# TensorE's order in a step of a two-layer graph network: half message sums between and behind the next pair's two groups of products

## The chip, the cores and the metric

The kernel runs on one core of a Trainium2 chip. The metric is the device time of one execution in microseconds; before the change it is 1939.5 us, the median of three runs (1931.52 to 1940.32). Engines are called PE (TensorE), ACT (ScalarE), DVE (VectorE), POOL (GpSimd) and SP (SyncE, which issues DMAs).

## The reference

There are 6250 nodes with 128 features and 100000 edges, sorted by target, with 16 features each. Two layers follow each other. Cut to what matters:

```
# layer one, over edges e = (src, dst)
m    = silu(concat(h[src], h[dst], edge_feat) @ W1 + b1) @ W2 + b2
agg  = segment_sum(m, dst)                       # per target node
hnew = silu(concat(h, agg) @ W3 + b3) @ W4 + b4
x1   = layernorm(x + (hnew + h))
# layer two
z    = (1 + eps) * x1 + segment_sum(x1[src], dst)
z    = relu(z @ V1 + c1) @ V2 + c2
y    = relu(layernorm(z + x1) * gamma + beta)
out  = layernorm(x1 + y)
```

## The kernel before

**Tiling.** Edges are cut into 196 groups of 512 (`GE`, four chunks `CH` of 128), and two groups make a pair: 98 pairs. A pair's targets lie within a window of 128 nodes (`PW`), because edges are sorted by target. A unit is 128 nodes; there are 48 units, the last one with two tiles. Layer one first computes the source term `x @ W1[:128] + b1` of all nodes and keeps it in HBM (`A_d`, "src_term"), so that an edge only has to fetch a row.

**A pair in layer one.** POOL gathers the source rows, one indirect DMA (`gather_rows`, L873) for each chunk: four for a group, eight for a pair. They go to a ring of eight group slots, `gath`; a slot is free when PE has read the group that was in it (`pool.wait_ge(pre_ps, done(g - RING))`, L888). The first four groups are gathered from `x` instead. DVE makes two one-hots: `terms_l` for target and edge features (`windows`, L1914, one instruction for each group, counted by `ohT_made`), and `oh` for the sums (`one_hots`, L1644). ACT fills the other halves of the operands (`edge_features`, L1006). PE adds up a group's inputs in a bank (`pre_sums`, L1224: four products L1233, then the gathered rows through a product with the identity, L1240), which it counts in `pre_ps`; ACT takes the SiLU of it (`messages`, L1017, counted by `msg_made`); PE sums the messages by target (`message_sums`, L1242: eight products L1250 into bank 2 or 3, then the degrees, L1252, counted by `sums_ps`); DVE adds the window into `S` (`add_sums`, L1927, instruction L1934).

[...]

**Steps.** Every engine runs the same staggered steps (`steps`, L477): in step s an engine does each of its stages for pair s minus the stage's lag, in the order in which the stages are listed. Four steps form a loop body; steps at the ends, and those that do something special, are written out. PE's list stands at L1514 to L1520: in step s it does `turn_ef` of pair s-1, `pre_sums` of pair s-2, then the early work, then `message_sums` of pair s-3, then the units' matmuls (`ordered_turn_x1`, `ordered_out0`, `ordered_hidden0`) for units whose targets are complete.

**Beside layer one.** Over steps 1 to 43 DVE also sorts the edges of the first 112 groups by source, with short transposes by PE (`turn_keys`). From step 45 on the early work begins: a part of layer two is done for tiles that are finished. PE has `early_sums` (L1396, target sums) and `early_rows` (L1383, choosing rows out of loaded windows), DVE `early_hots` (L1987 and L1993), SP the window loads.

**Units.** The unit's hidden layer, output, mean and variance (`rows0`, L2046: L2052, L2056, `stats`), inverse root and normalisation (L2036) follow 7 to 11 steps behind. ACT computes the root for all units but the last one, for which POOL computes it (`rsqrt0`, L913), queued behind all gathers. The rows go to HBM (`layer1_input`).

**The passage to layer two.** POOL gathers two more pairs' worth of rows ("bridge", 16 indirect DMAs) for finished tiles, then the last unit's root, and then waits until all of x1 is stored: `pool.wait_ge(x1_out, landed(NT - 1))` (L933). In layer two POOL gathers 42 pairs (336 indirect DMAs), PE chooses and sums rows (L1410, L1434, L1362) and does the node matmuls (L1441, L1456), and DVE builds one-hots, adds, and normalises.

**What PE waits for in the two stages at issue.** `pre_sums` waits for `efT_made` of the pair, for both windows of the pair (`ohT_made, done(2 * k + 1)`), for the SiLU that frees the bank (`msg_made, done(g - 2)`) and for the gathered rows. `message_sums` waits for the one-hots `oh_made`, for the addition two pairs before (`sums_added`), and for the messages of each half.

Of the kernel before, what the change touches and what calls it, by code (L numbers as in the profile page):

```python
# [14 lines left out]
D = 128  # L15
FE = 16
CH = 4
GE = CH * P
W = 64
PW = 2 * W  # L20
# [23 lines left out]
def done(n):  # L44

    return n + 1 + START
# [11 lines left out]
def build(nc, x, src, dst, ef, W1, b1, W2, b2, W3, b3, W4, b4, eps, V1, c1, V2, c2, gamma, beta, out):  # L58
# [36 lines left out]
    with ExitStack() as ctx:  # L95
        def sb(name, shape, dt=F32):
            return ctx.enter_context(nc.sbuf_tensor(name, shape, dt))
# [6 lines left out]
        def counter(name, engine):  # L104

            counters.setdefault(engine, []).append(sem(name))
            return counters[engine][-1]


        ident = sb("ident", [P, P])  # L110
# [83 lines left out]
        deg_col = sb("deg_col", [P, DEEP])  # L194
        ef_s = sb("ef_s", [P, 2, 2 * CH * FE])
        oh = sb("oh", [P, 2, 2 * CH, PW])
        pre = sb("pre", [P, CH * D])
        msg = sb("msg", [P, 4, CH * D])
# [14 lines left out]
        bank = [ctx.enter_context(nc.psum_tensor(f"bank{i}", [P, 512], F32)) for i in range(8)]  # L213
# [112 lines left out]
        ohT_made = counter("ohT_made", "dve")  # L326
        oh_made = counter("oh_made", "dve")
        xw_made = counter("xw_made", "act")
        ef_turned = counter("ef_turned", "pe")
        efT_made = counter("efT_made", "act")  # L330
        pre_ps = counter("pre_ps", "pe")
        msg_made = counter("msg_made", "act")
        sums_ps = counter("sums_ps", "pe")
        deg_added = counter("deg_added", "dve")
        sums_added = counter("sums_added", "dve")
# [78 lines left out]
        def of_pair(lag, body):  # L414

            return lag, NPAIR, body

        def of_unit(lag, body):

            def at_even(i, m, q):  # L420
                if m % 2 == 0:
                    body(i // 2 if isinstance(i, int) else q * 2 + m // 2)
            return lag, 2 * UNITS, at_even

        def of_early(lag, body):

            return lag + FIRST_EARLY, EARLY, body
# [94 lines left out]
        def at_steps(parts):  # L522

            return 0, NPAIR, only_at(parts)
# [99 lines left out]
        def of_unit_in(first, last, lag, body):  # L624

            count, _, part = last - first, None, of_unit(0, lambda j: body(first + j))[2]
            return lag + 2 * first, 2 * count, part
# [11 lines left out]
        UNITS = NT - 1  # L639
# [3 lines left out]
        FIRST_BEFORE = (FIRST_EARLY + 3 - 8) // 2  # L643
# [486 lines left out]
        def _(pe):  # L1130
            start_counters(pe, "pe")
            mm = nc.tensor.matmul
# [82 lines left out]
            def add_from_x(g, ps):  # L1215

                pe.wait_ge(from_x_kept, g + 1)
                for j in range(CH):
                    mm(ps[:, j * D:(j + 1) * D], gath[:, g, j * P:(j + 1) * P], wab[:, 0:D], start=False, stop=False)
                for j in range(CH):  # L1220
                    last = mm(ps[:, j * D:(j + 1) * D], ident[:, :], b1_bc[:, :], start=False, stop=j == CH - 1)
                last.then_inc(pre_ps, 1)

            def pre_sums(k, m, q):  # L1224

                u = m % 2
                pe.wait_ge(efT_made, done(k))
                pe.wait_ge(ohT_made, done(2 * k + 1))
                for h in range(2):
                    g = 2 * k + h  # L1230
                    pe.wait_ge(msg_made, done(g - 2))
                    for j in range(CH):
                        mm(bank[h][:, j * D:(j + 1) * D], terms_l[:, u, h, j, :], terms_r[:, u, h, j, :],  # L1233
                           start=j == 0, stop=False)
                    if isinstance(k, int) and k < FROM_X:
                        add_from_x(g, bank[h])
                        continue
                    slot = 2 * m + h
                    pe.wait_ge(gathered[slot], 16 * CH * (q + 1))
                    mm(bank[h][:, :], ident[:, :], gath[:, slot, :], start=False, stop=True).then_inc(pre_ps, 1)  # L1240

            def message_sums(k, m, q):  # L1242
                u = m % 2

                pe.wait_ge(oh_made, done(k))
                pe.wait_ge(sums_added, done(k - 2))
                for c in range(2 * CH):
                    if c % CH == 0:
                        pe.wait_ge(msg_made, done(2 * k + c // CH))
                    mm(bank[2 + u][:, 0:PW], msg[:, 2 * u + c // CH, c % CH * D:(c % CH + 1) * D], oh[:, u, c, :],  # L1250
                       start=c == 0, stop=c == 2 * CH - 1)
                mm(bank[2 + u][0:1, PW:2 * PW], deg_col[:, m:m + 1], ident[:, :],  # L1252
                   start=True, stop=True).then_inc(sums_ps, 1)

            def hidden0(j, turned, run=0):

# [243 lines left out]
            def any_order():  # L1500
                for x in range(BRIDGED):
# [10 lines left out]
                all_units1(pe, hidden1, out1)  # L1512

            steps(pe, NPAIR - 2, (4,) + TURNS + tuple(s + 1 for s in TURNS) + (SORTED, SORTED + 1),  # L1514
                  of_early(3, early_kept), of_pair(1, turn_ef), of_pair(2, pre_sums), of_early(3, early_sums),
                  of_early(2, early_rows), (0, NPAIR, keys_taken),
                  of_unit_in(FIRST_BEFORE, UNITS - 1, 9, hnew_read), of_pair(3, message_sums),
                  at_steps({4: weight_products, **{k + 1: lambda k=k: turn_from_x(k) for k in range(FROM_X)}}),
                  of_unit(10, ordered_turn_x1), *in_banks(8, ordered_out0), of_unit(7, ordered_hidden0),
                  (0, NPAIR, turn_keys))  # L1520
# [677 lines left out]
```

## Time and profile before

| what | value |
|---|---|
| median of three runs | 1939.5 us (1931.52, 1939.5, 1940.32) |
| span of the profiled execution | 1500.6 us |
| own time of the profiled execution | not given; the runs lie 430.9 to 439.7 us above the span |
| PE busy | 1285.9 us, 86% |
| POOL busy | 1107.0 us, 74% |
| DVE busy | 1014.5 us, 68% |
| ACT busy | 642.1 us, 43% |
| mean granted clock of PE | 0.945 of full speed |

The span runs from the first to the last instruction of the profiled execution; what lies around it in a timed run is start and end of the program. Layer one's loop takes up the span to about 1035 us, layer two the rest. A busy share counts an engine's instructions alone; matmuls are pipelined and their ends modelled, so that starts are firmer than ends. POOL's own rows are the indirect DMAs' issue: the gathered bytes land later. "issue" is idle time in which an engine waited for nothing that the profile shows.

### The profile page before, as it was taken

How to read it: one execution, taken by the hardware profiler on the slowest of the kernel's cores; microseconds unless marked ns; L12 is line 12 of the kernel's file. 1: busy time of each engine (PE TensorE's matmuls, PEld its weight loads, DVE VectorE, ACT ScalarE, POOL GpSimd, SP SyncE). 2: the span in 40 equal slices, each digit the busy share in tenths (PEclk: the TensorE clock that was granted, in tenths of full speed). 3: DMA queues.
4: the chain of work that ended last, by engine and by line, in shares of the span. 5: the costliest groups of instructions: out<-in, count | busy, mean ns of one | idle time of the engine just before them, and what ended most of it. 6: DMA issues, size and time to landing. Idle time of an engine off the chain costs nothing.

```text
span 1500.6 us, 31339 instructions
## 1 busy us (share of the span) xinstructions
PE 1285.9 (86%) x8165; PEld 1063.6 (71%) x8165; DVE 1014.5 (68%) x2310; ACT 642.1 (43%) x1257; POOL 1107.0 (74%) x1164
## 2 busy tenths in 40 slices
PE   6788789778777889888888888885999999999992
PEld 6666667556556667767767776764899999998982
DVE  4678888677665565665566656643666888878866
ACT  2744556555555555555556555551111111111111
POOL 5777777777777777777777777777777777777771
PEclk9898889999998999999999999997999999999996
DMA  6533333333336454454455445433887778778731
GB/s 206 135 85 92 93 95 94 95 96 91 95 90 119 118 138 125 126 136 131 125 131 133 125 128 135 113 80 105 258 261 230 208 230 241 222 230 241 213 92 47
DMA packets 189124, 214.15 MB, mean 143 GB/s; under 512 B 60426, under 2 KB 149517, under 8 KB 189011
## 3 DMA queue, kind: packets, MB, share of 16 engines
q1 hardware_dynamic: 138399, 131.62, 28.9%
q0 software_dynamic: 36352, 74.52, 21.3%
q10 hardware_dynamic: 14260, 6.68, 1.6%
q8 instruction: 49, 0.80, 0.2%
q14 instruction: 64, 0.52, 0.1%
HBM read 202.74 MB, written 9.85 MB: 142 GB/s over the span
## 4 chain that ended last, share of the span: by engine, by line
POOL 42%; PE 32%; issue 15%; DVE 4%; DMA 4%; SPq 1%; ACT 1%; DVEq 0%; ACTq 0%; POOLq 0%
POOL gath L873 42%; PE bank L1434 9%; PE bank L1410 8%; PE bank L1362 4%; DMA gath<-src_term,src_col 2%; PE bank L1240 2%; PE bank L1250 2%; PE bank L1233 2%; PE bank L1421 1%; DMA T<-in_x 1%; DMA gath<-layer_input,src_col 1%; PE bank L1396 1%; PE bank L1383 1%; PE bank L1441 0%; PE bank L1456 0%
## 5 line engine op out<-in xcount | busy, mean ns | idle before, releaser
L873 POOL DMA_INDIRECT gath<-src_term,src_col x768 | 737.2, 960 | 234.2 <-issue 230.2
L873 POOL DMA_INDIRECT gath<-layer_input,src_col x336 | 329.6, 981 | 105.6 <-issue 100.6
L1240 PE MATMUL bank<-gath,ident 128*128 128x512 f32 x384 | 218.3, 652 | 114.5 <-DMA gath<-src_term,src_col 113.8
L1233 PEld LDWEIGHTS bank<-terms_r,terms_l 128*128 128x128 f32 x1568 | 209.4, 201 | 83.1 <-issue 69.2
L1233 PE MATMUL bank<-terms_r,terms_l 128*128 128x128 f32 x1568 | 219.6, 286 | 30.4 <-ACT msg L1022 22.0
L1923 DVE TENSOR_SCALAR_CACHE_REDUCE terms_l<-dst_bc,node_col 64x512 f32<-64x512 int32 x196 | 221.0, 1128 | 13.1 <-issue 7.2
L1250 PEld LDWEIGHTS bank<-oh,msg 128*128 128x128 f32 x1568 | 198.7, 202 | 26.9 <-issue 26.1
L1934 DVE TENSOR_TENSOR S<-S,bank 128x128 f32 x98 | 28.1, 286 | 270.2 <-PE bank L1252 178.2
L1250 PE MATMUL bank<-oh,msg 128*128 128x128 f32 x1568 | 202.3, 285 | 0.0
L1434 PE MATMUL bank<-S 128*128 128x288 f32 x672 | 170.0, 406 | 0.1
L1649 DVE TENSOR_TENSOR oh<-bank,dst_rel 128x1024 f32<-128x1024 f32 x140 | 169.8, 1213 | 0.0
L1240 PEld LDWEIGHTS bank<-gath,ident 128*128 128x128 f32 x384 | 61.2, 201 | 129.7 <-DMA gath<-src_term,src_col 129.4
L1434 PEld LDWEIGHTS bank<-S 128*128 128x128 f32 x672 | 124.5, 190 | 31.1 <-issue 0.2
L1022 ACT ACTIVATE msg<-bank 128x512 f32<-128x512 f32 x196 | 115.8, 599 | 59.8 <-PE bank L1240 57.4
L1013 ACT COPY terms_l<-bank 64x512 f32<-64x512 f32 x196 | 113.7, 580 | 40.0 <-PE bank L1203 28.6
L1076 ACT COPY S<-bank 128x512 f32<-128x512 f32 x84 | 49.2, 586 | 185.8 <-PE bank L1410 181.8
L1993 DVE TENSOR_TENSOR S<-bank,dst_of 128x2304 f32<-128x2304 f32 x44 | 112.0, 2548 | 10.1 <-PE bank L1434 3.8
L1014 ACT COPY terms_r<-bank 64x512 f32<-64x512 f32 x196 | 113.4, 578 | 0.0
L1035 ACT ACT_TABLE_LOAD x48 | 61.6, 1283 | 66.9 <-DVE mv L2025 66.4
L1362 PE MATMUL bank<-oh,gath 128*128 128x128 f32 x672 | 84.4, 279 | 5.1 <-DMA gath<-layer_input,src_col 5.1
L1362 PEld LDWEIGHTS bank<-oh,gath 128*128 128x128 f32 x672 | 80.4, 195 | 5.7 <-DMA gath<-layer_input,src_col 5.7
L1987 DVE TENSOR_SCALAR xT<-xT,even_odd 128x1024 f32<-128x1024 f32 x84 | 60.5, 762 | 5.4 <-DMA xT<-sorted_src 5.4
(219 smaller groups left out, 1754.7 us busy)
## 6 DMA issues: line engine op xcount, KB each, us to landing
dst_bc<-in_dst SPq DMA_DIRECT2D x195, 128.0 KB
xT<-sorted_src SPq DMA_DIRECT2D x42, 512.0 KB
xs<-layer_input SPq DMA_DIRECT2D x136, 128.0 KB
gath<-src_term,src_col POOLq DMA_INDIRECT x768
terms_l<-layer_input SPq DMA_DIRECT2D x88, 128.0 KB
terms_r<-layer_input SPq DMA_DIRECT2D x88, 128.0 KB
msg<-layer_input SPq DMA_DIRECT2D x80, 128.0 KB
ef_s<-in_edge_attr SPq DMA_DIRECT2D x97, 64.0 KB
```

The costliest lines, as they stand in the source:

```text
L873: g.indirect_dma_start(out=to[:, j * D:(j + 1) * D], out_offset=None, in_=table[0:rows, :], in_offset=bass.IndirectOffsetOnAxis(ap=indices ...
L1013: a.copy(terms_l[r, u, h, :, :], bank[4][r, 0:P].unsqueeze(1).to_broadcast([W, CH, P]))
L1014: last = a.copy(terms_r[r, u, 1 - h, :, :], bank[4][r, P:2 * P].unsqueeze(1).to_broadcast([W, CH, P]))
L1022: a.activation(msg[:, 2 * (m % 2) + h, :], bank[h][:, :], ACT.Silu).then_inc(msg_made, 1)
L1233: mm(bank[h][:, j * D:(j + 1) * D], terms_l[:, u, h, j, :], terms_r[:, u, h, j, :], start=j == 0, stop=False)
L1240: mm(bank[h][:, :], ident[:, :], gath[:, slot, :], start=False, stop=True).then_inc(pre_ps, 1)
L1250: mm(bank[2 + u][:, 0:PW], msg[:, 2 * u + c // CH, c % CH * D:(c % CH + 1) * D], oh[:, u, c, :], start=c == 0, stop=c == 2 * CH - 1)
L1362: last = mm(bank[2 + u][:, 0:PW], gath[:, s, c % CH * D:(c % CH + 1) * D], oh[:, u, c, :], start=c == 0, stop=c == 2 * CH - 1)
L1410: last = mm(bank[h][:, c * D:(c + 1) * D], src_hot[:, u, w, e], x_near[m][h * CH + c][:, w, :], start=w == 0, stop=w == 1)
L1434: last = mm(bank[4][:, 0:DW], rows_kept[:, c // CH, c % CH * D:(c % CH + 1) * D], dst_hot[:, u, c, :], start=o % LATE == 0 and c == 0, sto ...
L1649: ve_.tensor_tensor(oh[:, u, :, :], iota_ps.unsqueeze(1).to_broadcast(shape), dst_rel[:, ds((k + first) * (2 * CH), 2 * CH)].unsqueeze(2). ...
L1923: ve_.tensor_scalar(terms_l[r, u, h, :, :], dst_bc[r, u, :].rearrange("n (p j) -> n j p", j=CH), node_col[r, ds(k, 1)], None, ALU.is_equal ...
```

## The change

In `message_sums` the eight products of a pair are split into two bodies, one for each half (group) of the pair, and so is `pre_sums`, one for each group. The order in a step becomes: `pre_sums` of group 0, the early work, half 0 of the sums of the pair before, `pre_sums` of group 1, half 1 of these sums with the degrees. The waits go along: `efT_made` is now waited for by each of the two groups; a group waits for its own window only (`ohT_made, done(g)`); `oh_made` and `sums_added` stand before half 0. The matmuls and their operands are the same.

```diff
-            def pre_sums(k, m, q):
-                u = m % 2
-                pe.wait_ge(efT_made, done(k))
-                pe.wait_ge(ohT_made, done(2 * k + 1))
-                for h in range(2):
+            def pre_sums(h):
+                def body(k, m, q):
+                    u = m % 2
                     g = 2 * k + h
+                    pe.wait_ge(efT_made, done(k))
+                    pe.wait_ge(ohT_made, done(g))
                     pe.wait_ge(msg_made, done(g - 2))
...
-            def message_sums(k, m, q):
-                u = m % 2
-                pe.wait_ge(oh_made, done(k))
-                pe.wait_ge(sums_added, done(k - 2))
-                for c in range(2 * CH):
-                    if c % CH == 0:
-                        pe.wait_ge(msg_made, done(2 * k + c // CH))
-                    mm(bank[2 + u][:, 0:PW], msg[:, 2 * u + c // CH, c % CH * D:(c % CH + 1) * D], oh[:, u, c, :],
-                       start=c == 0, stop=c == 2 * CH - 1)
-                mm(bank[2 + u][0:1, PW:2 * PW], deg_col[:, m:m + 1], ident[:, :],
-                   start=True, stop=True).then_inc(sums_ps, 1)
+            def message_sums(h):
+                def body(k, m, q):
+                    u = m % 2
+                    if h == 0:
+                        pe.wait_ge(oh_made, done(k))
+                        pe.wait_ge(sums_added, done(k - 2))
+                    pe.wait_ge(msg_made, done(2 * k + h))
+                    for j in range(CH):
+                        mm(bank[2 + u][:, 0:PW], msg[:, 2 * u + h, j * D:(j + 1) * D], oh[:, u, h * CH + j, :],
+                           start=h == 0 and j == 0, stop=h == 1 and j == CH - 1)
+                    if h == 1:
+                        mm(bank[2 + u][0:1, PW:2 * PW], deg_col[:, m:m + 1], ident[:, :],
+                           start=True, stop=True).then_inc(sums_ps, 1)
+                return body
...
-                  of_early(3, early_kept), of_pair(1, turn_ef), of_pair(2, pre_sums), of_early(3, early_sums),
+                  of_early(3, early_kept), of_pair(1, turn_ef), of_pair(2, pre_sums(0)), of_early(3, early_sums),
                   of_early(2, early_rows), (0, NPAIR, keys_taken),
-                  of_unit_in(FIRST_BEFORE, UNITS - 1, 9, hnew_read), of_pair(3, message_sums),
+                  of_unit_in(FIRST_BEFORE, UNITS - 1, 9, hnew_read), of_pair(3, message_sums(0)),
+                  of_pair(2, pre_sums(1)), of_pair(3, message_sums(1)),
```

## Rows read from the trace of the kernel before

**Rows 1.** The page: busy time of the engines, and the chain that ended last

```profile
PE 1285.9 (86%) x8165; PEld 1063.6 (71%) x8165; DVE 1014.5 (68%) x2310; ACT 642.1 (43%) x1257; POOL 1107.0 (74%) x1164
...
POOL 42%; PE 32%; issue 15%; DVE 4%; DMA 4%; SPq 1%; ACT 1%; DVEq 0%; ACTq 0%; POOLq 0%
```

**Rows 2.** Waits of POOL, whole span: total us, times, longest

```profile
POOL gath L873 <- issue: 335.4, 1100, 0.3
...
POOL gath L873 <- PE bank L1240: 4.0, 13, 0.3
POOL gath L873 <- DMA layer_input<-ot: 3.5, 1, 3.5
```

**Rows 3.** Stretches, gathers alone: length, POOL busy (count), granted clock, DMA share, GB/s

```profile
900.00:1000.00 100.00, 75.91 (x80) 0.98 0.44 115
...
1100.00:1200.00 100.00, 76.18 (x78) 1.00 0.78 232
```

**Rows 4.** Timeline of POOL, layer one's ends: start, duration [idle before <-releaser]

```profile
22.49 1.15 POOL L873 DMA_INDIRECT xs<-in_x,src_col  x1 [5.89 <-DVE src_col L1536]
...
1013.41 1.01 POOL L873 DMA_INDIRECT gath<-src_term,src_col  x1 [0.30 <-issue]
...
1033.73 0.96 POOL L873 DMA_INDIRECT gath<-layer_input,bridge_rows  x1 [0.30 <-issue]
1034.72 0.25 POOL L918 TENSOR_SCALAR var_eps<-mv 128x2 f32<-128x2 f32 x1
...
1039.28 1.08 POOL L873 DMA_INDIRECT gath<-layer_input,src_col  x1 [3.49 <-DMA layer_input<-ot]
```

**Rows 5.** Timeline of PE, one step of layer one

```profile
802.66 1.05 PE L1233 MATMUL bank<-terms_r,terms_l 128*128 128x128 f32 x8
804.97 1.13 PE L1240 MATMUL bank<-gath,ident 128*128 128x512 f32 x2 [1.25 <-DMA gath<-src_term,src_col]
805.93 1.13 PE L1396 MATMUL bank<-src_rows_f,As 128*128 128x288 f32 x4
806.90 1.05 PE L1383 MATMUL bank<-xs,xTs 128*128 128x128 f32 x8
807.79 1.95 PE L1250 MATMUL bank<-oh,msg 128*128 128x128 f32 x16
809.67 0.38 PE L1252 MATMUL bank<-ident,deg_col 128*1 128x128 f32 x2
```

**Rows 6.** Timelines of PE and POOL, where the ring of gather slots is tightest

```profile
80.17 1.78 PE L1240 MATMUL bank<-gath,ident 128*128 128x512 f32 x2
...
93.78 0.96 POOL L873 DMA_INDIRECT gath<-src_term,src_col  x1 [0.30 <-issue]
```

**Rows 7.** Waits of PE, whole span

```profile
PE bank L1240 <- DMA gath<-src_term,src_col: 113.8, 71, 10.6
```

**Rows 8.** Timeline of all engines, end of layer one

```profile
1016.11 1.29 PE L1240 MATMUL bank<-gath,ident 128*128 128x512 f32 x2 [3.17 <-DMA gath<-src_term,src_col]
1017.19 3.46 PE L1250 MATMUL bank<-oh,msg 128*128 128x128 f32 x16
...
1031.98 0.25 DVE L2025 BATCH_NORM_AGGREGATE mv<-st 128x2 f32<-128x6 f32 x2
```

**Rows 9.** Timelines of POOL and DVE, two gathers longer than most

```profile
177.31 1.26 POOL L873 DMA_INDIRECT gath<-src_term,src_col  x1 [0.30 <-issue]
...
177.45 0.28 DVE L2052 SCALAR_TENSOR_TENSOR v<-xt,b_bc 128x128 f32<-128x128 f32 x1
...
810.98 0.61 DVE L1987 TENSOR_SCALAR xTs<-As,even_odd 128x256 f32<-128x256 f32 x2
...
811.12 1.05 POOL L873 DMA_INDIRECT gath<-src_term,src_col  x1 [0.30 <-issue]
```

**Rows 10.** Timelines of PE and POOL, first neighbour sums of layer two

```profile
1071.36 1.95 PE L1362 MATMUL bank<-oh,gath 128*128 128x128 f32 x16
...
1080.70 0.95 POOL L873 DMA_INDIRECT gath<-layer_input,src_col  x1 [0.30 <-issue]
```

More of the change, by code:

```diff
@@ L1236, in pre_sums @@
                         add_from_x(g, bank[h])
-                        continue
+                        return
                     slot = 2 * m + h
@@ L1240, in pre_sums @@
                     mm(bank[h][:, :], ident[:, :], gath[:, slot, :], start=False, stop=True).then_inc(pre_ps, 1)
-            def message_sums(k, m, q):
-                u = m % 2
-                pe.wait_ge(oh_made, done(k))
-                pe.wait_ge(sums_added, done(k - 2))
-                for c in range(2 * CH):
-                    if c % CH == 0:
-                        pe.wait_ge(msg_made, done(2 * k + c // CH))
-                    mm(bank[2 + u][:, 0:PW], msg[:, 2 * u + c // CH, c % CH * D:(c % CH + 1) * D], oh[:, u, c, :],
-                       start=c == 0, stop=c == 2 * CH - 1)
-                mm(bank[2 + u][0:1, PW:2 * PW], deg_col[:, m:m + 1], ident[:, :],
-                   start=True, stop=True).then_inc(sums_ps, 1)
+                return body
[12 more added lines that the diff above has]
+                           start=True, stop=True).then_inc(sums_ps, 1)
+                return body
             def hidden0(j, turned, run=0):
```

## The prediction

> **What bounds the kernel now.** I read the page first. Its busy shares point at TensorE: PE is busy 86% of the span, POOL 74%. The chain that ended last says otherwise: POOL holds 42% of it, PE 32% [rows 1], and "issue" 15%. So the question is which of the two would let the other go faster, and that is asked stage by stage.
>
> POOL's waits come second. Of its idle time, 335.4 us in 1100 pieces is "issue", the fixed 0.3 us between two gathers; only 4.0 us in 13 pieces is put down to PE, and none of those is over 0.3 us, the fixed gap again [rows 2]. The reader is to see that POOL never stands still for PE in layer one.
>
> The stretches confirm it: 80 gathers in 100 us of layer one [rows 3]. POOL's timeline gives the whole stage: the first gather starts at 22.49 and the last of the bridge ends at 1033.73 + 0.96 = 1034.69, after 800 gathers (16 from x, 768 of the source term, 16 of the bridge) [rows 4]. That is 1012.2 us / 800 = 1.265 us each, against 0.96 + 0.30 = 1.26 for one undisturbed gather. POOL is a conveyor that runs without a stop from before layer one's loop until layer two opens. A pair is 8 gathers, 10.1 us.
>
> PE's own waits are the mirror image: 113.8 us in 71 pieces before L1240, for gathered rows [rows 7]. PE is ahead of its supply and waits for the conveyor.
>
> Then layer two. After the last bridge gather POOL makes the last unit's inverse root (L918 at 1034.72), VectorE normalises, the rows are stored, and the next gather starts at 1039.28, released by that store [rows 4]. Nothing before that moment but POOL's queue sets it: the variance that POOL needs was ready at 1031.98 + 0.25 = 1032.23 [rows 8], 2.46 us before POOL came free.
>
> **The change, part by part.** In a step TensorE now does: products and gathered rows of group 0 of pair k; the early work; sums of half 0 of pair k-1; products and rows of group 1 of pair k; sums of half 1 of pair k-1 and the degree row.
>
> *Matmuls.* None is added or removed. Per pair there remain 16 products, 4 rows instructions, 16 sum instructions and 2 for the degree; half a message sum is 1.95 / 2 = 0.98 us [rows 5].
>
> *Waits.* Today a pair's products and sums issue 6 + 4 = 10 waits, then 8 + 4 = 12. Two more per step are not shown anywhere as work. The lower bound is 0. The upper bound is, by the nearest row, POOL's pause of 0.30 at each gather [rows 4]: 0.6 us a step. I take 0, because PE stands 1.25 us in that step before the gathered rows of group 1 [rows 5], and 0.6 fits in it. Without that cover it would be at most 98 x 0.6 = 59 us; PE's total wait of 113.8 [rows 7] is larger.
>
> *Order in a steady step* [rows 5]. Now PE finishes group 1's products by 803.7, waits until the rows land at 804.97, and only then does rows (0.96 start to start), early sums and early rows (0.97 + 0.89), message sums (1.88) and degree (0.38): 5.08 us behind the landing, at 810.05. Then the early work and 0.98 of sums stand ahead of the wait, and behind the landing come only 0.96 + 0.98 + 0.38 = 2.3 us. VectorE's addition of the sums is released some 2.8 us sooner. PE's work per 10.1 us stays the same, so the same 1.25 us is left over and still ends with a landing. The step's period is the conveyor's. Worth at the end of the span: 0.
>
> *Group 1 of a pair is read later when PE is not waiting for rows.* Its slot and its bank come free behind early work and half a sum: 0.97 + 0.89 + 0.98 = 2.8 us later in the step. Queued behind: POOL's gather eight groups later, ScalarE's SiLU of that group, and VectorE's windows. The ring has eight groups, and the tightest place I found is at group 14: its gather starts at 93.78, the read that freed its slot (group 6's) ended at 80.17 + 1.78 = 81.95 [rows 6], 11.83 us earlier. 2.8 us uses a quarter of that, so POOL does not notice: 0. Lower bound 0 as well, for POOL has nothing to gain from a slot freed sooner.
>
> *Narrower waits.* Group 0's products now need only the first window one-hot of the pair, not both, but half 0 of the sums, and with it group 1, needs pair k-1's one-hots, which stand behind both windows in VectorE's queue. The one gives PE about a window, the other takes about that back. All of it lies under the ring's 11.83 us. 0.
>
> *The tail.* The last layer-one rows land at 1016.11; behind them stand L1240 (1.29) and the sums of pair 96 (3.46, against 1.95 in the steady step) [rows 8, 5]. Half of the latter moves ahead into the 3.17 us that PE waited: 0.98 to 1.73 us sooner for the variance that POOL takes. It is already 2.46 us early, so the gain is 0, and the margin becomes about 4 us. If instead all of the tail's matmuls ran as slowly as these sums, the variance could come late, and what exceeds 2.46 us would count; I allow 0 to 2 us.
>
> *Layer two.* Its code is the same. POOL's first slot wait there has 1080.70 - (1071.36 + 1.95) = 7.39 us to spare [rows 10], and POOL again issues 78 gathers in 100 us [rows 3]. Nothing to gain or lose but the start.
>
> **A rule that speaks against the change.** POOL's time per gather isn't quite constant. The gather at 177.31 took 1.26 us with L2052, a VectorE instruction on two SBUF inputs, beginning inside it; the one at 811.12 took 1.05 with L1987 beginning 0.14 before it [rows 9]; the usual is 0.96. The whole excess in layer one is small: 1034.69 - 22.49 - 800 x 1.26 = 4.2 us. The change moves VectorE's instructions against the gathers. [...] Bounds from rows: all excess gone, -4.2 us; every one of the 49 units' L2052 costing 1.26 - 0.96 = 0.30 and every one of the 48 early steps' L1987 costing 0.09, 14.7 + 4.3 = +19 us. I take 0, since the phase is as arbitrary after as before.
>
> **Sum.** 0 (matmuls) + 0 (waits) + 0 (order) + 0 (ring) + 0 (tail) + 0 (layer two) on a span of 1500.6 us. No time of its own is given with the profiled execution; the three timed runs lie 1931.5 - 1500.6 = 430.9 to 439.7 us above its span. So a span of 1500.6, and 1939.5 us against the median.
>
> **Rivals.**
> *PE is the bound* (faster). For it: 86% busy, and the 71 waits before L1240. If each of these hid a half sum of 0.98 us that is serial today, 71 x 0.98 = 69.6 us, 1870 us. Against it: POOL's gaps never exceed 0.3 us, so no gather could start earlier.
> *Gathers stretched by VectorE* (slower). The mechanism above; its addition follows the landing at a new phase, which repeats every pair, so a bad phase would repeat too. Full price +19 us, 1958.5; from half of that on (9.7 us) it decides. Against: 800 gathers show 4.2 us in all.
> *The ring runs dry* (slower). In the steps with the sort, VectorE and PE are late by themselves, and if the new order lengthened a step by 0.5 us over the 40 steps up to about 460 us, 20 us of lag less 11.83 of slack would be 8 us on POOL, 1947.7; over 0.54 us a step it passes 9.7. Against: PE's total is unchanged and its results for VectorE come sooner.
> That the change doesn't do what it says is excluded: the two halves stand in TensorE's program order.
>
> **Numbers.** About 0.5%, 9.7 us, is what a measurement can tell from no change; the three runs alone spread 8.8 us. Forecast 0.88. PE-bound 0.03. Stretched gathers 0.04. Ring 0.02. A shift that no row explains 0.03, of which faster 0.02. Stretching and ring are slower by over 0.5% in most of their cases; together with the unexplained: faster 0.05, same 0.88, slower 0.07. Range: from the lowest run less 1.5, 1930, up to 1946, which is the highest run plus some 6 us of stretching.
>
> **What would show it.** Right: 80 gathers per 100 us from 100 to 1000 us, no POOL gap over 0.31 before the store of layer one's last rows, the last bridge gather ending near 1034.7, layer two's first gather near 1039.3; L1250 in two blocks of 8 per step; the addition L1934 some 2 to 3 us nearer the landing; PE's wait before L1240 similar in sum. Wrong: POOL waiting on PE for over 0.3 us at a time, many gathers over 1.0 us, or L918 starting later than POOL came free.

## The result, and the profile after

The changed kernel takes 1878.4 us (median of 4 runs, 1873.41 to 1883.44) beside 1937.2 us (median of 4, 1931.52 to 1940.32) of the kernel before: a ratio of 0.972, with a 95% interval from 0.969 to 0.975. The forecast was 1939.5 us and no change.

The first thing to see lies outside the rows. The profiled execution of the changed kernel took 1873.41 us by its own time and has a span of 1871.5 us: they differ by 1.9 us. The trace of before has a span of 1500.6 us, while its timed runs take 1931.5 to 1940.3. If the same 1.9 us hold for the kernel before, the missing 431 to 440 us never lay around the span, and that trace is of another kind of execution of the same program. The next section shows that this is so: a long execution of the kernel before has a span of 1942.8 us in a time of 1944.7. I call the two kinds *short* (about 1500 us) and *long* (about 1900 us).

The page of the changed kernel, a long execution (busy us and share, then the chain that ended last), answers to [rows 1]:

```profile
PE 1446.5 (77%) x8165; PEld 1158.7 (62%) x8165; DVE 1016.3 (54%) x2310; ACT 630.6 (34%) x1257; POOL 1103.6 (59%) x1164
...
another core or an unknown queue 27%; issue 21%; PE 20%; DVE 20%; DVEq 7%; ACT 3%; SPq 1%; ACTq 1%; DMA 1%; POOLq 0%; POOL 0%
```

Its waits of POOL over the span (us in total, times, longest) answer to [rows 2]:

```profile
POOL gath L873 <- issue: 287.5, 938, 0.9
POOL gath L873 <- remote: 203.3, 119, 3.4
POOL gath L873 <- PE bank L1366: 122.2, 37, 24.6
POOL gath L873 <- PE bank L1240: 50.2, 24, 4.5
```

Its gathers alone by stretch (length, POOL busy and count, granted clock, DMA share, GB/s) answer to [rows 3]:

```profile
200.00:300.00 100.00, 62.94 (x67) 0.73 0.27 75
900.00:1000.00 100.00, 60.45 (x64) 0.92 0.37 103
1500.00:1600.00 100.00, 63.45 (x65) 0.96 0.61 182
```

And POOL's timeline where layer two opens answers to [rows 4]:

```profile
1267.14 0.23 POOL L918 TENSOR_SCALAR var_eps<-mv 128x2 f32<-128x2 f32 x1 [18.75 <-DVE mv L2030]
...
1271.68 1.08 POOL L873 DMA_INDIRECT gath<-layer_input,src_col  x1 [3.49 <-DMA layer_input<-ot]
```

From 900 to 1000 us a gather still takes 60.45 / 64 = 0.94 us, but there are 64 in 100 us and not 80. POOL is no longer a conveyor: 50.2 us of waiting for L1240 in 24 pieces of up to 4.5 us, where [rows 2] has 4.0 us in 13 pieces of 0.3, and 203.3 us in 119 pieces for "remote", a releaser that the trace doesn't name. Layer two's first gather starts at 1271.68, against 1039.28 in [rows 4]. PE's busy sum has grown from 1285.9 to 1446.5 us with the same 8165 instructions. Nothing of this can be put down to the change, because the two traces are of different kinds. For that a long trace of the kernel before was needed.

### The profile page after: what moved, and what is told of

The parts are those of the page before. It is cut to its first block, busy times and chain, and to the rows that moved or that the text cites. A ratio compares the mean times of both kernels' runs of the same rounds, so it can differ in the third digit from the quotient of the medians.

```text
span 1871.5 us, 31423 instructions
## 1 busy us (share of the span) xinstructions
PE 1446.5 (77%) x8165; PEld 1158.7 (62%) x8165; DVE 1016.3 (54%) x2310; ACT 630.6 (34%) x1257; POOL 1103.6 (59%) x1164
## 4 chain that ended last, share of the span: by engine, by line
another core or an unknown queue 27%; issue 21%; PE 20%; DVE 20%; DVEq 7%; ACT 3%; SPq 1%; ACTq 1%; DMA 1%; POOLq 0%; POOL 0%
DVEq L1934 5%; DVE terms_l L1928 4%; PE bank L1438 4%; DVE oh L1654 4%; PE bank L1252 3%; PE bank L1414 2%; PE bank L1233 2%; PE bank L1240 2%; DVE bank L1741 2%; DVE src_rows_f L1745 1%; PE bank L1366 1%; DVE src_rows_f L1749 1%; ACT S L1076 1%; DVE st L2025 1%
## 5 line engine op out<-in xcount | busy, mean ns | idle before, releaser
L1252 PEld LDWEIGHTS bank<-oh,msg 128*128 128x128 f32 x1568 | 234.9, 219 | 152.4 <-issue 120.1
L1233 PE MATMUL bank<-terms_r,terms_l 128*128 128x128 f32 x1568 | 256.2, 307 | 63.9 <-issue 48.3
L1252 PE MATMUL bank<-oh,msg 128*128 128x128 f32 x1568 | 242.4, 303 | 61.9 <-issue 35.7
L1233 PEld LDWEIGHTS bank<-terms_r,terms_l 128*128 128x128 f32 x1568 | 228.2, 219 | 71.4 <-issue 69.7
L1240 PE MATMUL bank<-gath,ident 128*128 128x512 f32 x384 | 229.1, 678 | 14.2 <-issue 13.9
L1022 ACT ACTIVATE msg<-bank 128x512 f32<-128x512 f32 x196 | 113.5, 596 | 324.3 <-remote 229.2
L1438 PE MATMUL bank<-S 128*128 128x288 f32 x672 | 194.7, 448 | 25.1 <-ACT S L1076 22.0
L1438 PEld LDWEIGHTS bank<-S 128*128 128x128 f32 x672 | 138.6, 212 | 72.2 <-issue 32.6
L1366 PE MATMUL bank<-oh,gath 128*128 128x128 f32 x672 | 104.3, 290 | 57.0 <-issue 55.3
L1387 PE MATMUL bank<-xs,xTs 128*128 128x128 f32 x384 | 66.6, 328 | 80.9 <-issue 55.2
L1387 PEld LDWEIGHTS bank<-xs,xTs 128*128 128x128 f32 x384 | 59.8, 234 | 100.5 <-issue 98.5
L1240 PEld LDWEIGHTS bank<-gath,ident 128*128 128x128 f32 x384 | 68.4, 219 | 26.2 <-issue 26.1
```

The costliest lines, as they stand in the source:

```text
L1022: a.activation(msg[:, 2 * (m % 2) + h, :], bank[h][:, :], ACT.Silu).then_inc(msg_made, 1)
L1252: mm(bank[2 + u][:, 0:PW], msg[:, 2 * u + h, j * D:(j + 1) * D], oh[:, u, h * CH + j, :], start=h == 0 and j == 0, stop=h == 1 and j == CH ...
L1366: last = mm(bank[2 + u][:, 0:PW], gath[:, s, c % CH * D:(c % CH + 1) * D], oh[:, u, c, :], start=c == 0, stop=c == 2 * CH - 1)
L1387: last = mm(rows_early_ps[:, c * D:(c + 1) * D], hot_early[:, u, w, c * P:(c + 1) * P], near_early[:, u, c, w, :], start=w == 0, stop=w == 1)
L1438: last = mm(bank[4][:, 0:DW], rows_kept[:, c // CH, c % CH * D:(c % CH + 1) * D], dst_hot[:, u, c, :], start=o % LATE == 0 and c == 0, sto ...
```

## The comparison in long executions: where the 59 us lie

Both kernels ran again, unchanged. The first time they met only short executions (`b_again` and `a_again`, below). The second time, on another chip, both were long.

> The kernel before, unchanged, on another chip. If the long executions (1937 us) belong to a chip or to a stretch of time, this run can meet them: then its time is near 1937, its span lies within 3 us of its time, and its trace shows how its TensorE stalls, late releases and gathers stand against those of the changed kernel's long execution. Otherwise it comes out at 1499 to 1503 us as the runs so far, and the cause of the 0.972 stays open.

> The changed kernel, unchanged, beside b_third. Where before takes 1937, both theories of a gain that belongs to the long executions expect 1870 to 1885 (ratio 0.97). Where before takes 1500, all theories expect 1499 to 1503 (ratio 0.999 to 1.001).

Measured: before 1944.7 us in this run, with a span of 1942.8, and 1941.79 in the median of the 7 runs beside it (1938.53 to 1950.03). The changed kernel takes 1886.22 (median of 4, 1881.4 to 1891.17), a ratio of 0.9717 [0.9675, 0.9759]. The gain repeats, and it belongs to long executions.

The page of the kernel before in its long execution (as above):

```profile
PE 1466.9 (76%) x8165; PEld 1174.0 (60%) x8165; DVE 1019.0 (52%) x2310; ACT 631.4 (32%) x1257; POOL 1100.5 (57%) x1164
...
another core or an unknown queue 28%; PE 25%; issue 20%; DVE 12%; ACT 6%; DVEq 3%; SPq 2%; ACTq 2%; DMA 1%; POOLq 0%; POOL 0%
```

Its gathers by stretch:

```profile
200.00:300.00 100.00, 64.42 (x67) 0.83 0.28 76
900.00:1000.00 100.00, 55.50 (x58) 0.91 0.35 96
1500.00:1600.00 100.00, 60.27 (x63) 0.95 0.59 175
```

Those of the changed kernel, beside it on the same chip:

```profile
200.00:300.00 100.00, 64.66 (x67) 0.86 0.28 76
900.00:1000.00 100.00, 62.27 (x66) 0.94 0.40 108
1500.00:1600.00 100.00, 59.65 (x62) 0.95 0.59 174
```

Read the three lines as three stages. From 200 to 300 us, before there is any early work, both issue 67 gathers. In layer two both are alike, 63 and 62. From 900 to 1000 the kernel before issues 58 and the changed one 66. Counted by the degree rows, one burst for each pair: pairs 3 to 42 take 12.08 us each before and 12.10 after; pairs 48 to 92 take 13.83 before and 12.29 after, 44 x 1.54 = 68 us. Pair 48 comes at 670 before and at 676 after, the last pair at 1322 and 1264; from there to the end both need 621 and 617 us. So the gain is made in the steps that have early work (64 us from pair 48 to the last one), and outside them little changes: 6 us are lost ahead of pair 48 and 4 gained behind the last pair.

What TensorE waits for in that stretch (engine, instruction, releaser: us in total, times, longest), first of the kernel before, 700 to 1300 us:

```profile
PE bank L1201 <- issue: 45.5, 18, 5.1
PE bank L1233 <- issue: 39.9, 49, 1.9
PE bank L1201 <- ACT As L1068: 34.2, 7, 6.3
```

Then of the changed kernel, 700 to 1250 us:

```profile
PE bank L1387 <- issue: 40.2, 25, 2.8
PE bank L1233 <- issue: 27.9, 48, 1.2
...
PE bank L1387 <- ACT terms_r L1014: 9.6, 6, 6.1
...
PE bank L1201 <- issue: 0.5, 2, 0.3
```

L1201 is the first matmul of a step. Ahead of it TensorE's program has `early_kept`, a wait for ScalarE's copy (L1068) of the early rows that TensorE itself made in the step before: the copy must be done before their bank is written again. Before, 34.2 + 45.5 = 79.7 us pass there (I count "issue" in, as a releaser of which the trace has no record, for long executions have few records of signals, see the end; for a single wait that is not shown). After, 0.5 us. One such step of the kernel before, in TensorE's timeline (start, duration, instruction [idle before <-releaser]; each product of these lines is two rows in the trace, so x16 is eight products):

```profile
887.63 0.27 PE L1233 MATMUL bank<-terms_r,terms_l 128*128 128x128 f32 x1 [0.45 <-issue]
...
891.18 1.13 PE L1383 MATMUL bank<-xs,xTs 128*128 128x128 f32 x8
892.15 1.95 PE L1250 MATMUL bank<-oh,msg 128*128 128x128 f32 x16
...
894.98 0.48 PE L1262 MATMUL bank<-T,cdeg 1*128 x2
901.40 0.47 PE L1201 MATMUL bank<-ident,ef_s 128*128 128x128 f32 x1 [5.94 <-ACT As L1068]
```

and ScalarE's copy between them:

```profile
900.78 0.37 ACT L1068 COPY As<-bank 128x256 f32<-128x256 f32 x1 [5.36 <-remote]
```

The early rows (L1383) end at 891.18 + 1.13 = 892.31. ScalarE then has other work until 895.42, stands idle for 5.36 us and starts the copy only at 900.78, 8.47 us after the rows. The trace also records when a semaphore was counted, and it has the count of these rows at 900.75: what came late is the signal. Behind the rows TensorE has the message sums, the degree row and a unit's matmuls, which last until 894.98 + 0.48 = 895.46. Then it stands 5.94 us. In the changed kernel the same part of a step reads:

```profile
889.73 1.13 PE L1387 MATMUL bank<-xs,xTs 128*128 128x128 f32 x8 [0.79 <-issue]
...
892.48 1.02 PE L1240 MATMUL bank<-gath,ident 128*128 128x512 f32 x2
...
895.28 0.48 PE L1266 MATMUL bank<-T,cdeg 1*128 x2
895.98 0.30 PE L1201 MATMUL bank<-ident,ef_s 128*128 128x128 f32 x1 [0.22 <-issue]
```

```profile
894.70 0.37 ACT L1068 COPY As<-bank 128x256 f32<-128x256 f32 x1
```

The early rows (L1387) end at 889.73 + 1.13 = 890.86 and are copied at 894.70, 3.84 us later; their count stands at 893.72, 2.86 us behind them, and ScalarE had a SiLU to finish first. Group 1's products and rows (the second line is its L1240) and the halves of the sums now lie behind them, so that TensorE is busy until 895.28 + 0.48 = 895.76 and waits 0.22 us. The cover behind the early rows was 895.46 - 892.31 = 3.15 us and is 895.76 - 890.86 = 4.90, which is 1.75 us more: one group's products and rows, 891.59 to 893.35.

Theory K, formed from this: in long executions a signal of TensorE reaches its reader late (from the end of the early rows to the copy: median 3.0 and up to 8.5 us before, 1.9 and up to 5.3 after, over 48 steps each, against a median of 0.04 in the short execution of before). The early rows' way to ScalarE and back is then longer than what TensorE has to do meanwhile, and the loop of the two sets the step. The new order would help because it moves the early rows ahead by a group.

Theory K is not the whole of it, and two readings of the same traces show that. The first is ScalarE's waits (us in total, times, longest). The kernel before, 700 to 1300 us:

```profile
ACT As L1068 <- remote: 122.7, 22, 9.7
ACT msg L1022 <- remote: 2.7, 1, 2.7
```

The changed kernel, 700 to 1250 us:

```profile
ACT msg L1022 <- remote: 200.7, 54, 7.8
ACT As L1068 <- remote: 5.6, 1, 5.6
```

ScalarE waited for the early rows before and waits for a group's gathered rows (the SiLU, L1022) after. The recorded counts say the same: from pair 48 to 94, the count of group 0's rows (L1240) stands a median of 0.01 us behind their end before, and 4.85 us after. So the new order does not only put more work behind a late signal; other signals are late in it. Why, no run shows.

The second reading is where TensorE stands idle for over 0.3 us, from the degree row of pair 48 to that of the last pair, by the idle times that the profile gives. These pauses sum up to 155 us before and 109 after, while the stretch is 652 us long before and 588 after. At the head of the step (L1201) 89.0 us became 0.3. But before the early rows (L1383, now L1387) 3.8 became 51.5, and before the early sums (L1396, now L1400) 18.1 came up from nothing: of the 89 us some 66 came back there. At the products and gathered rows (L1233 and L1240) 55.9 became 30.2, most of it inside bursts in which nothing is waited for. The other 18 us of the 64 are no pauses: TensorE's instructions themselves take up 19 us less (494 and 475). So the head of the step, less what came back, is 23 us of 64, about a third.

## The experiments

Theory L, the first, said that a shorter loop of TensorE is what pays when TensorE is the bound. Theory S said that late signals of TensorE in general favour the new order. Their rival was that nothing but noise or the condition differs.

**Both kernels unchanged, first time.** No edit.

> The kernel before, unchanged, for a second profile. Theory of the prediction (the profiled execution shown is what is timed, and 439 us lie outside its span): span near 1500 us, POOL without a gap over 0.31 us in layer one, and a time near 1937 us. Theory B (the timed executions run otherwise than the one whose trace was read; the changed kernel's span lies only 1.9 us under its time): span near 1935 us, about 12.9 us per pair in layer one against 10.1, POOL standing still at the first gather of each group for a freed slot, additions of the sums (L1934) starting 3 to 5 us behind the degree row (L1252) where the first trace has 0.14.

> The changed kernel, unchanged, beside the others on one chip. Both theories: 1873 to 1884 us, span 2 us less, 12.3 us per pair in steady steps of layer one, ratio 0.972.

Measured: `b_again` 1499.06 us with a span of 1497.2, and before 1500.64 (25 runs, 1498.4 to 1503.59); `a_again` 1500.55 (10 runs), a ratio of 1.0004 [0.9994, 1.0013]. No theory had expected these times. In short executions the change is worth nothing. POOL's waits in `a_again`:

```profile
POOL gath L873 <- issue: 338.5, 1111, 0.3
...
POOL gath L873 <- PE bank L1366: 1.2, 4, 0.3
```

1111 pauses of the fixed 0.3 us, and not one for L1240: the conveyor of the forecast, unchanged by the new order.

**Parts of the change.** `c_waits` has the split bodies and waits in the old order; `c_whole` puts group 1 behind both halves.

```diff
 c_waits: pre_sums(0), pre_sums(1), early_sums, early_rows, ..., message_sums(0), message_sums(1)
 c_whole: pre_sums(0), early_sums, early_rows, ..., message_sums(0), message_sums(1), pre_sums(1)
```

> Split bodies with the waits of the change, but in the order of before: group 0, group 1, early work, half 0, half 1. If the narrower waits (a group's own window) make the gain: 1878 us, ratio 0.97. If the order makes it: 1937 us, ratio 1.00 within 0.003.

> Group 1 behind both halves of the message sums, which stay together: group 0, early work, half 0, half 1 with degrees, group 1. If the gain comes from the two groups being apart (ScalarE, POOL and VectorE get one result each half step): about the changed kernel's 1878 us or better, ratio 0.97 or less. If it comes from sums standing on both sides of group 1: at most half of it, 1905 us or more. If my conveyor were the bound: 1937.

Measured: 1501.17 (ratio 1.0002 [0.9993, 1.0012]) and 1500.45 (1.0004 [0.9995, 1.0014]). Both were short executions, in which none of these orders matters. They say nothing of the long ones.

**POOL's bound taken away.** Two of the four chunks of a group are gathered, and the other two are left out, so that half of the gathered rows are stale.

```diff
-                for j in range(CH):
+                for j in range(chunks):
...
-                    gather_rows(A_d, N, g % RING, src_col[:, g * CH:(g + 1) * CH], gathered[g % RING])
+                    gather_rows(A_d, N, g % RING, src_col[:, g * CH:(g + 1) * CH], gathered[g % RING], chunks=2)
```

> The kernel before, but in layer one POOL gathers only two of a group's four chunks, so that half of the gathered rows are stale: it leaves out half of the gathers, which makes the conveyor 5.05 us per pair. PE's own work, about 8.8 us a pair, and the loops between the engines are then the bound. Both theories: layer one some 100 to 130 us shorter, 1370 to 1410 us where the kernel before takes 1500.

> The changed kernel with the same half of the gathers left out. Theory L (the new order shortens the loop between PE and the engines that wait for it, and this is hidden only where POOL is the bound): 0.6 us a pair less than the other, which is what 1937 against 1878 us makes, so about 50 to 60 us below it. Theory P (the order is worth nothing to PE's throughput; its gain needs signals of PE that arrive late): within 8 us of it.

Measured: 1368.16 us in the old order (ratio 0.9119 [0.9103, 0.9134]), 1391.43 in the new one (0.9267 [0.925, 0.9285]). The old order comes out just under the expected 1370 to 1410. With TensorE's side as the bound the new order is 23 us *slower*, which neither theory expected. A pair takes 8.63 against 8.99 us (pairs 48 to 92, from the degree rows). TensorE's waits in the new order, 500 to 850 us, hold one that the old order doesn't have:

```profile
PE bank L1400 <- DVE T L1962: 11.9, 9, 1.4
```

The early sums (L1400) wait for VectorE (L1962), now that they come one group's work sooner. That is the price side of the same move, and from pair 48 to 92 most of it: TensorE stands idle 0.29 us a pair there in the new order and never in the old one. Theory L falls.

**TensorE lengthened.** Every L1233 and L1250 product is made twice.

```diff
-                    for j in range(CH):
-                        mm(bank[h][:, j * D:(j + 1) * D], terms_l[:, u, h, j, :], terms_r[:, u, h, j, :],
+                    for again_ in range(2):
+                        for j in range(CH):
+                            mm(bank[h][:, j * D:(j + 1) * D], terms_l[:, u, h, j, :], terms_r[:, u, h, j, :],
```

> The kernel before with each product of L1233 and L1250 made twice, which doubles these terms: 32 more rows of 0.11 us a pair, 3.5 us, so that PE needs 12.3 us a pair against POOL's 10.1. Both theories: 1700 to 1740 us, with POOL standing still for freed slots in layer one.

> The changed kernel with the same products made twice. Theory L: 40 to 60 us below the other one. Theory P: within 8 us, for PE is then busy without a pause in either order.

Measured: 1640.13 (1.093 [1.091, 1.095]) and 1641.61 (1.0944 [1.0925, 1.0963]), both below the 1700 to 1740 that were expected: a pair takes the expected 12.2 us from pair 48 to 92, but only 10.4 from pair 3 to 42, where there is no early work yet. TensorE is the bound where there is, and POOL waits for it in 78 places of `p_old`:

```profile
POOL gath L873 <- PE bank L1241: 136.4, 78, 2.8
```

Yet the order is worth nothing. From pair 48 to 92 TensorE has no idle gap in either order, and a pair takes 12.19 us in both, as theory P said; theory L falls again.

**Three signals late.** The counts `ef_turned`, `pre_ps` and `sums_ps` go by SyncE, which reads TensorE's own count, moves 64 bytes, waits for them and only then counts (`ef_turned` without the 64 bytes).

```diff
+            def relay(raw, out, per_pair, h, turn):
+                def body(k, m, q):
+                    sp.wait_ge(raw, done(per_pair * k + h))
+                    if turn is not None:
+                        sp.dma_start(relayed[:, :], x[0:1, 0:16]).then_inc(relay_in, 16)
+                        sp.wait_ge(relay_in, relay_count(k, turn))
+                    sp.sem_inc(out, 1)
+                return body
```

> The kernel before, with TensorE's signals in layer one made late: the counts of L1203, L1240 and the degree row go to SyncE, which passes them on; ahead of passing on a group's rows or a pair's sums it makes a 64 byte DMA and waits for it, some 2 us. Matmuls, gathers and order are the kernel's own. Theory S (what the recorded times of 1937 and 1878 us have in common is late signals of TensorE, and the old order suffers more from them): a pair takes over 10.1 us, POOL stands still for freed slots, 1550 to 1950 us. Theory N (late signals are hidden by the ring of eight groups): 1500 to 1520.

> The changed kernel with the same late signals. Theory S: 0.3 to 0.9 us a pair less than the old order with them, 30 to 90 us below it. Theory N, or if the new order only takes cover away, as with half of the gathers (+23 us): level with it or slower.

> Late signals with group 1 behind both halves of the sums. Under theory S the distance between the two groups is what helps: within 15 us of the changed order with late signals. If half 1 behind group 1 is what matters (sums signalled late in the step): slower than that by 20 us or more, or faster, for the sums are signalled before group 1.

> Late signals with the order of before and the split waits. If the narrower waits matter there: clearly below the old order with late signals. If only the order does: within 5 us of it.

Measured: old order 1705.48 (ratio 1.136 [1.1341, 1.1379]), new order 1823.47 (1.2153 [1.2133, 1.2173]), group 1 behind both halves 1881.41 (1.2532 [1.2507, 1.2557]), split waits in the old order 1705.36 (1.1369 [1.1351, 1.1388]). Theory S falls, in the direction opposite to what it said: the later in a step group 1 stands, the slower. The narrower waits are worth nothing (`r_waits`). ScalarE's waits from 500 to 850 us show where the new order loses. Old order:

```profile
ACT terms_l L1033 <- SPq L834: 144.2, 24, 7.1
```

New order:

```profile
ACT terms_l L1033 <- SPq L834: 118.9, 20, 6.5
ACT msg L1042 <- SPq L834: 90.9, 21, 5.4
```

The second line is new: the SiLU (L1042 here) waits 90.9 us in 21 pieces for the relayed count, now that group 1 stands behind the early work. So a late count of `pre_ps` seems to speak for the old order; the three signals were made late together, so that none of them has a price of its own. And the one signal that theory K names, `rows_ps`, was not late here at all. The `r_` kernels are therefore no likeness of a long execution: in the long trace of before the early rows' count is late and that of group 0's rows is not. A kernel with all of TensorE's signals late together was not run.

**The early rows' signal alone.** Two edits. `d_early` moves only the early work: it stands ahead of group 1, and the message sums stay whole behind it. `e_old`, `e_new` and `e_early` make `rows_ps` late for ScalarE's copy in the three orders.

```diff
 d_early: pre_sums(0), early_sums, early_rows, pre_sums(1), ..., message_sums(0), message_sums(1)

+            def relay_rows(e, m, q):
+                sp.wait_ge(rows_ps, done(e))
+                for i in range(3):
+                    sp.dma_start(relayed[:, :], x[0:1, 0:16]).then_inc(relay_in, 16)
+                    sp.wait_ge(relay_in, 16 * (3 * e + i + 1))
+                sp.sem_inc(rows_late, 1)
...
-                act.wait_ge(rows_ps, done(e))
+                act.wait_ge(rows_late, done(e))
```

> Only the early work is moved: TensorE does group 0, the early sums and early rows, then group 1, and behind it both halves of the message sums, unsplit. Theory K (the early rows' way to ScalarE and back closes a loop: TensorE's next step begins with a wait for ScalarE's copy of the rows of this step, and in the order before only sums, degree and unit matmuls lie between): where before takes 1940, this takes 1878 to 1892, as the changed kernel does, for the 1.75 us of group 1 then lie between too. Rival H (the half sums between the groups are what helps): 1935 to 1945 there. Where before takes 1500, both expect 1499 to 1503, and the kernels beside this one decide.

> The order before, with one signal made late: the early rows' count reaches ScalarE's copy only after SyncE has moved 64 bytes three times and waited for each, some 6 us. Where before takes 1500: theory K expects TensorE to stand about 6.4 - 3.5 = 2.9 us at the head of each of 48 steps, a pair to take 8.64 + 2.9 = 11.5 us instead of 10.1, and the time to be 1550 to 1590. The rival H puts no price on this signal: what it costs here it costs in all three orders alike.

> The order of the change, with the same late signal. Theory K: 5.25 us of TensorE's work lie behind the early rows instead of 3.5, so it stands 1.2 us a step at most, 9.8 us a pair is under the gathers' 10.1, and the time stays at 1500 to 1515, 40 us or more under e_old. If the order does not matter for this signal, it equals e_old within 5 us.

> The order of d_early (only the early work ahead of group 1, sums unsplit), with the same late signal. Theory K: like e_new, 1500 to 1515, within 6 us of it. Rival H: like e_old.

Measured, all in short executions (before 1501.0): `d_early` 1500.76 (0.9996 [0.9986, 1.0005]); `e_old` 1531.81 (1.0203 [1.0186, 1.022]); `e_new` 1516.67 (1.0091 [1.0069, 1.0114]); `e_early` 1516.67 (1.0103 [1.0086, 1.012]). One late signal costs the old order 31 us and the new one 16. `e_early`, in which the sums aren't interleaved at all, has the same median as `e_new`. So K holds and H falls for this signal in short executions. The sizes were missed: `e_old` lies below its 1550 to 1590, `e_new` 1.7 us above its 1500 to 1515, and the difference of 15 us between the orders is about a third of the 40 expected. The delay was mis-sized. In `e_old` the early rows end at 813.65 and the copy starts at 817.78:

```profile
812.60 1.05 PE L1392 MATMUL bank<-xs,xTs 128*128 128x128 f32 x8
...
818.40 0.30 PE L1210 MATMUL bank<-ident,ef_s 128*128 128x128 f32 x1 [2.17 <-ACT As L1077]
```

```profile
817.78 0.37 ACT L1077 COPY As<-bank 128x256 f32<-128x256 f32 x1 [6.75 <-SPq L833]
```

That is 4.13 us (median of the 48: 4.0), not 6.4; three round trips took less than I had taken them for. TensorE's waits from 550 to 1000 us, in the order `e_old`, `e_new`, `e_early`:

```profile
PE bank L1210 <- ACT As L1077: 71.1, 41, 2.4
```

```profile
PE bank L1261 <- DVE v L2070: 34.9, 21, 3.5
PE bank L1409 <- DVE T L1971: 23.1, 10, 2.6
PE bank L1210 <- ACT As L1077: 8.3, 17, 1.2
```

```profile
PE bank L1210 <- ACT As L1077: 36.9, 37, 2.2
PE bank L1409 <- DVE T L1971: 16.4, 9, 2.9
```

The head of the step (L1210 here) costs 71.1, 8.3 and 36.9 us. What remains in `e_new` are new waits for VectorE at the sums (L1261) and at the early sums (L1409), 34.9 and 23.1 us; `e_early` has less of both and more at the head. The medians of the two agree, but these two traces are of executions of 1521.3 and 1513.8 us, so that the lines are not to be set off against each other to the us. That SyncE's relay also held back its own loads, and with them VectorE, would explain the new waits and was not measured apart.

## Why the prediction was wrong

**The step that failed is the sum.** It adds six zeros "on a span of 1500.6 us", puts the runs "430.9 to 439.7 us above its span", and carries that distance over as a constant, because "what lies around it in a timed run is start and end of the program". Every execution whose own time is known shows 1.8 to 2.3 us between the two, short or long (1499.06 and 1497.2 in `b_again`, 1944.7 and 1942.8 in `b_third`, 1873.41 and 1871.5 after). Measured were 1878.4 beside 1937.2 us, 59 us where the sum had 0. A timed run 29% above the span said that the trace was not of an execution like the timed ones, and with it fell the ground under every term.

**"POOL is a conveyor that runs without a stop"** holds where it was read. In short executions the change is worth nothing (1.0004 [0.9994, 1.0013]), and most signs that were to show the forecast right are there in `a_again`: POOL has no wait for L1240, the last bridge gather ends at 1033.14, and layer two's first gather starts at 1037.89, 1.4 us from the 1039.28 of [rows 4]. In the long execution of before (`b_third`) it is false: 58 gathers in 100 us, and 182.5 us of POOL's waits for L1240 in 45 pieces.

**"2.8 us uses a quarter of that"**, of the ring's slack: the slack was 11.83 us in the trace of before; in the long execution of before a gather starts 0.27 us behind the read that frees its slot at the tightest places, such as group 104's at 653.05. The ring has no slack left there, and what TensorE loses POOL loses too.

**"Order in a steady step"** worked out what comes behind the landing of the gathered rows. It counted the early work as something that moves ahead of that wait, and asked who waits for the sums, which come 2.8 us sooner. It did not ask who waits for the early rows. The wait is in the listed stages (`early_kept`), and the trace of before shows no row of it, because the copy started a median of 0.04 us behind the rows there. With the rule "name who waits for each moved result" it would have been found, with a price only for a late signal.

**The rivals.** *PE is the bound* gave 1870 us, near the 1878 measured, and that is luck: it priced half sums hidden under waits for gathered rows. With TensorE as the bound the new order gains nothing (`p_`) or loses 23 us (`g_`). *The ring runs dry* named the right queue with the wrong sign. *Gathers stretched by VectorE* took no part: a gather takes 0.94 to 0.96 us in every stretch of the long traces shown. Its upper price of 0.30 us for each L2052 was too high by the trace of before itself: during 48 of the gathers an L2052 ran (there are 48 of them, not 49), and these took 0.98 us on average, 0.02 more than the usual.

**What stays open.** Theory K is shown in short executions for one signal that was made late, and is worth 15 us there. For the long executions it is only read from the traces, and by them it covers about a third of the gain. `d_early` met only short ones, so rival H, that the half sums between the groups are what helps, is not excluded where the gain is made. How much of the 0.972 comes from the early rows' place, how much from the pauses inside bursts that also shrank, and why other signals are late in the new order, is not settled. Nor is it known what makes an execution long.

## What to carry to other kernels

Compare the span of the profiled execution with the timed runs before anything else. Here they differ by some 2 us where they belong together; where they differed by 431 to 440, the trace was evidence on another kind of execution, and "no change" couldn't be forecast from its slack. For every block of work that is moved, list each reader of its result, also those that come back to the same engine: an engine that waits for a copy of what it made in the step before has a loop whose cover is the work in between, and that cover is what a reordering changes. Moving work ahead of such a wait also takes cover from whatever feeds it (the 23 us of `g_new`), so the same order can gain, cost or do nothing according to what bounds.

## What the runs showed of the hardware

- The same program took about 1500 us in four sets of runs on three chips, and about 1940 us in the timed runs of the first record and in one set on a fourth chip. Within a set of the experiments it never changed from one to the other. Only in the first record, whose trace is short and whose timed runs are long, do both kinds stand side by side.
- In the long executions TensorE's signals are late and the others' are not. By the trace's records of when a semaphore was counted, all 887 counts of TensorE that are found in the short trace of before stand 0.01 us behind the end of their instruction. In the long one 660 are found, a median of 3.5 us behind and 421 of them by over 1 us, while of ScalarE's 419 none is over 1 us late and of VectorE's 920 only 14.
- The late counts come in bunches. In the long trace of before, the counts of five instructions that ended between 882.78 and 886.17 us stand from 888.46 to 888.69. In that of the changed kernel they are often some 6.2 us apart: ScalarE, VectorE and POOL are released together at 899.15, 899.37 and 899.39, and ScalarE again at 905.42 and 911.50.
- In the long executions TensorE also pauses inside bursts, at instructions that wait for no semaphore: 186 idle gaps of over 0.3 us, 166 us in all, in the long trace of before, such as the 0.45 us before the product at 887.63 above; 142 to 166 gaps and 116 to 142 us after. The short traces of both orders have none.
- The gathers themselves are untouched: 0.94 to 0.96 us each in both kinds. The trace of the changed kernel's first long execution holds 10199 records of semaphore updates, the short one of before 37454, which may be why so much in it is put down to "remote" or "issue".
- The granted clock in the long stretch from 900 to 1000 us was 0.91 before and 0.94 after, against 0.98 in [rows 3], with TensorE pausing more. TensorE's instructions sum up to 1466.9 us instead of 1285.9; how much of that is clock and how much is pauses inside bursts wasn't separated.
